# First cross attention: the output projection moves to the mix's PSUM bank, and a tile's order on three engines is changed

## The reference, cut to what matters

```python
x = x + tanh(g_xattn[1]) * _L1_xattn_ref(_layernorm(x), ctx, ctx, mask, wq, bq, wk, bk, wv, bv, wo, bo)

def _L1_xattn_ref(q, k, v, mask, wq, bq, wk, bk, wv, bv, wo, bo):   # 16 heads of 8
    qh, kh, vh = (split_heads(a @ w.T + b) for a, w, b in ((q, wq, bq), (k, wk, bk), (v, wv, bv)))
    corr = einsum('bhqd,bhkd->bhqk', qh, kh) / sqrt(8)
    corr = where(row_mask, corr, -1e9)          # a masked row gets even weights
    hidden = einsum('bhqk,bhkd->bhqd', softmax(corr), vh)
    return hidden.reshape(B, S, 128) @ wo.T + bo
```

## Time and profile before

| | us |
|---|---|
| median of 3 runs (3789.99 to 3798.97) | 3791.75 |
| the profiled execution's own time | 3789.1 |
| its span in the profile | 3787.0 |
| TensorE matmul busy | 3182.0 (84%) |
| VectorE busy | 2670.9 (71%) |
| ScalarE busy | 1691.3 (45%) |
| GpSimd busy | 1309.2 (35%) |

### The profile page before, as it was taken

One profiled execution on the slowest core, in us unless ns is written; L12 is line 12 of the kernel. 1 busy time (PEld: TensorE's weight loads), 2 busy tenths in 40 slices (PEclk: granted clock), 3 DMA queues, 4 the chain that ended last, 5 costly groups with the idle time before them and its releaser, 6 DMA issues. The chain is left out here.

```text
span 3787.0 us, 91181 instructions
## 1 busy us (share of the span) xinstructions
PE 3182.0 (84%) x31627; PEld 2212.8 (58%) x31627; DVE 2670.9 (71%) x5541; ACT 1691.3 (45%) x3176; POOL 1309.2 (35%) x1592
## 2 busy tenths in 40 slices
PE   3687999998888893699859997489999778999886
PEld 1465787886666441566646664256666445666644
DVE  7666555555788779788766666778887547888655
ACT  1232223222777355555512223256666225666521
POOL 1664100000233000144310003078887108898710
PEclk8776999999999996799959999799999899999998
DMA  4211000000000015011000002200000110000011
GB/s 134 65 43 52 0 0 0 0 0 5 14 14 14 1 58 208 16 46 45 28 17 1 0 0 66 62 13 10 9 10 4 36 30 12 10 9 9 9 33 55
DMA packets 164346, 107.86 MB, mean 28 GB/s; under 512 B 91486, under 2 KB 153100, under 8 KB 163212
## 3 DMA queue, kind: packets, MB, share of 16 engines
q1 hardware_dynamic: 162652, 104.02, 9.3%
q10 hardware_dynamic: 1584, 2.44, 0.2%
HBM read 68.52 MB, written 16.78 MB: 23 GB/s over the span
## 5 line engine op out<-in xcount | busy, mean ns | idle before, releaser
L2478 POOL TENSOR_TENSOR la_turned<-la_turned,la_sines 128x1024 f32<-128x1024 f32 x128 | 301.8, 2358 | 152.3 <-DVE la_sines L2406 149.4
L2398 DVE TENSOR_TENSOR la_turned<-A,la_cos 128x1024 f32<-128x1024 f32 x128 | 156.8, 1225 | 163.6 <-ACT la_sq L2377 146.9
L2472 POOL TENSOR_TENSOR la_scaled<-la_turned,la_rlen 128x1024 f32<-128x1024 f32 x128 | 243.6, 1903 | 16.9 <-POOL la_rlen L2465 13.4
L916 PE MATMUL B<-l0f_mixed,l0f_sums 128*128 128x256 f32 x768 | 176.2, 379 | 0.0
L1386 POOL COPY l1x_vd<-half 128x16 f32<-128x16 f32 x8 | 1.2, 212 | 490.9 <-POOLq L48 490.9
L2715 ACT ACTIVATE gg_gate<-B,gg_b 128x512 f32<-128x512 f32 (+1 forms) x96 | 65.9, 686 | 211.6 <-PE B L2741 211.6
L2509 PEld LDWEIGHTS A<-ident,la_scaled 128*128 128x128 f32 x1024 | 119.9, 141 | 66.0 <-issue 65.7
L916 PEld LDWEIGHTS B<-l0f_mixed,l0f_sums 128*128 128x128 f32 x768 | 145.9, 190 | 19.8
L2524 PE MATMUL A<-la_wq,la_hT 128*128 128x512 f32 x256 | 148.4, 662 | 10.9 <-DVE la_sines L2406 10.9
L1717 POOL TENSOR_SCALAR l3x_factor<-l3x_raw 128x256 f32<-128x256 int32 x16 | 13.8, 864 | 398.3 <-DMA l3x_raw<-in_l3x_mask 397.1
L2411 DVE TENSOR_REDUCE la_length<-la_sq 128x16 f32<-128x1024 f32 x128 | 151.0, 1180 | 0.0
(11 more groups left out here) (465 smaller groups left out, 9215.3 us busy)
## 6 DMA issues: line engine op xcount, KB each, us to landing
l1f_spill<-l1f_work SPq DMA_DIRECT2D x16, 768.0 KB, 3.3
l1f_xT<-l1f_spill SPq DMA_DIRECT2D x16, 768.0 KB, 6.0
l2x_ctx<-in_ctx SPq DMA_DIRECT2D x128, 64.0 KB, 2.2
memory_vd<-vd SPq DMA_DIRECT2D x64, 68.0 KB
X<-in_x SPq DMA_DIRECT2D x4, 1024.0 KB, 6.2
gates_rows<-in_ctx_rows SPq DMA_DIRECT2D x16, 256.0 KB, 2.9
memory_ctxT<-in_ctxT SPq DMA_DIRECT2D x64, 64.0 KB, 1.8
l1x_ctxT<-in_ctxT SPq DMA_DIRECT2D x64, 64.0 KB
```

What stands on the lines that cost most here:

```text
L916: last = pe.matmul(bank[:, o * H:o * H + H], weights[:, k, o * P:o * P + P], x[:, k], start=(k == 0), stop=(k == 1))
L2398: dve.tensor_tensor(heads(turned[j % 2][:]), made_heads, cos[:, :, None, :].broadcast_to([P, 2, HEADS3, W3]), ALU.mult)\
L2472: pool.tensor_tensor(by_head(scaled), by_head(turned), spread_heads(rlen[j % 2][:], W3), ALU.mult)\
L2478: pool.tensor_tensor(turned[j % 2][:], turned[j % 2][:], sines[j % 2][:], ALU.add)\
```

## The change

y_out moves from `inputs` to `mixes`, behind turned_o. The waits that kept project_o and update apart from x_in, k_out and v_out go (update on q_set, set_q on out_done, turn_x on added, project_o on values). In their place the mix of a tile waits until the update of the tile before it is done (`added`, `done(it, j, 1)`), as both are now at the bank `mixes`. The order of a step becomes:

- TensorE: scores t, turn_o t-3, turn_x t+2, make_kv t+2, project_o t-3, turn_p t-1, mix t-2, project_q t+2.
- VectorE: outputs t-3, shift t, update t-3, measure t-3, norm_x t+3.
- ScalarE: copy_o t-3, copy_x, set_k and keep_v t+2, copy_p t-1, set_q t+2, exps t.

```diff
--- before.py
+++ after.py
@@ -1353,7 +1353,7 @@
         turned_p, mixes, inputs = m.B[0], m.B[1][:, 0:CH], m.B[1][:, CH:2 * CH]
         out = mixes[:, 0:G * NW].rearrange("p (h w) -> p h w", h=H)
         if projected:
-            turned_o, y_out = mixes[:, G * NW:G * NW + P], inputs[:, P:2 * P]
+            turned_o, y_out = mixes[:, G * NW:G * NW + P], mixes[:, G * NW + P:G * NW + 2 * P]
         else:
             turned_o, y_out = inputs[:, P:2 * P], inputs[:, 2 * P:3 * P]
         x_in, k_out, v_out = inputs[:, 0:P], inputs[:, P:2 * P], inputs[:, 2 * P:3 * P]
@@ -1448,8 +1448,6 @@
                     t = it * 4 + j
                     dve.wait_ge(out_done, done(it, j))
                     dve.wait_ge(moved, done(it, j))
-                    if projected:
-                        dve.wait_ge(q_set, ahead(it, j, 5))
                     dve.scalar_tensor_tensor(m.X[:, t, :], y_out, m.tanh_g[:, gate_at:gate_at + 1], m.X[:, t, :],
                                              ALU.mult, ALU.add).then_inc(added, 1)
 
@@ -1480,12 +1478,12 @@
 
                 def step(it, j):
                     if projected:
-                        at4(it, j, -4, update)
+                        at4(it, j, -3, outputs)
                     at4(it, j, 0, shift)
+                    at4(it, j, -3, update)
                     if not projected:
-                        at4(it, j, -3, update)
-                    at4(it, j, -2, outputs)
-                    at4(it, j, -4 if projected else -3, measure)
+                        at4(it, j, -2, outputs)
+                    at4(it, j, -3, measure)
                     at4(it, j, 3, norm_x)
 
                 steps4(dve, step)
@@ -1530,7 +1528,6 @@
                     act.wait_ge(q_made if projected else turned, done(it, j))
                     act.wait_ge(scored, done(it, j, 2))
                     if projected:
-                        act.wait_ge(out_done, done(it, j, 5) if not isinstance(it, int) else max(done(it, j, 5), BEFORE))
                         act.activation(qT[j % 2][:], x_in, ACT.Identity, bias=bq[:]).then_inc(q_set, 1)
                     else:
                         act.copy(qT[j % 2][:], x_in).then_inc(q_set, 1)
@@ -1541,16 +1538,16 @@
 
                 def step(it, j):
                     at4(it, j, -3, copy_o)
-                    if not projected:
-                        at4(it, j, 2, set_q)
-                    at4(it, j, -1, copy_p)
                     if projected:
                         at4(it, j, 2, copy_x)
                         at4(it, j, 2, set_k)
                         at4(it, j, 2, keep_v)
+                        at4(it, j, -1, copy_p)
+                        at4(it, j, 2, set_q)
+                    else:
+                        at4(it, j, 2, set_q)
+                        at4(it, j, -1, copy_p)
                     at4(it, j, 0, exps)
-                    if projected:
-                        at4(it, j, 2, set_q)
 
                 steps4(act, step)
 
@@ -1589,7 +1586,8 @@
                 def turn_x(it, j):
                     pe.wait_ge(normed_x, done(it, j))
                     pe.wait_ge(q_set, done(it, j, 1))
-                    pe.wait_ge(added, done(it, j, 6) if not isinstance(it, int) else max(done(it, j, 6), BEFORE))
+                    if not projected:
+                        pe.wait_ge(added, done(it, j, 6) if not isinstance(it, int) else max(done(it, j, 6), BEFORE))
                     pe.transpose(x_in, xn[j % 2][:], m.ident[:]).then_inc(turned, 1)
 
                 def make_kv(it, j):
@@ -1610,6 +1608,8 @@
                 def mix(it, j):
                     pe.wait_ge(values, done(it, j))
                     pe.wait_ge(o_copied if projected else o_done, done(it, j, 1))
+                    if projected:
+                        pe.wait_ge(added, done(it, j, 1))
                     pe.wait_ge(p_copied, done(it, j))
                     for g in range(G):
                         for b in range(2):
@@ -1620,7 +1620,8 @@
 
                 def project_o(it, j):
                     pe.wait_ge(o_copied, done(it, j))
-                    pe.wait_ge(values if projected else q_set, ahead(it, j, 5))
+                    if not projected:
+                        pe.wait_ge(q_set, ahead(it, j, 5))
                     pe.wait_ge(added, done(it, j, 1))
                     pe.matmul(y_out, oT[j % 2][:], wo[:], start=True, stop=True).then_inc(out_done, 1)
 
@@ -1635,16 +1636,16 @@
                 def step(it, j):
                     at4(it, j, 0, scores)
                     at4(it, j, -3, turn_o)
-                    if not projected:
-                        at4(it, j, 2, turn_x)
+                    at4(it, j, 2, turn_x)
+                    if projected:
+                        at4(it, j, 2, make_kv)
+                        at4(it, j, -3, project_o)
                     at4(it, j, -1, turn_p)
-                    if projected:
-                        at4(it, j, 2, turn_x)
-                        at4(it, j, 2, make_kv)
                     at4(it, j, -2, mix)
                     if projected:
                         at4(it, j, 2, project_q)
-                    at4(it, j, -3, project_o)
+                    else:
+                        at4(it, j, -3, project_o)
 
                 steps4(pe, step)
```

## The result

The changed kernel takes 3889.47 us, the median of 4 runs (3886.32 to 3891.37), against 3791.32 before: a ratio of 1.0254, with a 95% interval of 1.0236 to 1.0272. The forecast was 3857 with a range of 3834 to 3880. So it is slower, as forecast, but by 98 us and not by 65, and 9 us outside the range.

A forecast was written before the change was run, and what follows sets the result against it. TensorE's queue plus its 0.76 us wait for keep_v set the 4.79 us step; the new closed chain adds 1.05 over 59 steps (62 us), the end about 3: +65, forecast 3857 us, range 3834 to 3880.

The forecast's parts named there:

- The chain: Scores, maximum, subtraction, update, mix, keep_v, project_q, scores: 5.84 us a tile against 4.79, 62 us over 59 steps.
- The handover to the mix: From VectorE's update to TensorE's mix: TensorE starts 0.05 us after VectorE's end, as turn_o did after L1444.
- The clock: Rival 2, TensorE's clock falls in the stage: 71 us more, 3928; chance 0.10 in whole or part.
- a clock lower for a fifth of the time: Partial case of rival 2 in the changed stage: total 3871 us; within rival 2's chance of 0.10.
- The end: Step 62 and last two passes, where mix through update no longer overlap: about 3 us more.
- about 1: In step 62 the scores of 63 wait for update and mix too: about 1 us.
- Rival 1: ScalarE's chain alone sets the step at 5.4 to 5.7 us: about 3840; chance 0.08.
- Rivals 3 and 4: 3: wait met early, VectorE's freed 0.75 counts, 3756, chance 0.03; 4: new waits fall into idle time, about 3792, 0.02.
- What was hidden: Outputs ahead of shift, measure, norm_x, turn_x, make_kv, project_o: covered by waiting; outputs would add 0.54 a tile if uncovered.
- VectorE's freed 0.75: Update no longer waits for set_q, freeing 0.75 us a step; alone worth nothing, VectorE then waits for scores.
- The rule on the bank: Mix and update may not be at one bank at once, so the wait stays and 5.84 stands.

The follow-up runs named there:

- The added instruction: Changed kernel with one more VectorE tensor_scalar (128x128, to an unread tile) between subtraction and update: 3909.51 us, ratio 1.0303.
- the wait order: Changed kernel with the mix's wait for the update put behind its wait for copy_p: 3876.83 us, ratio 1.0220.
- The second of the kernels with mix early: Kernel before, TensorE's mix moved ahead of turn_x, make_kv, turn_p, project_q; ScalarE copy_p, set_q, exps: 3838.96 us, ratio 1.0125.
- the fill: Changed kernel with the first four of turn_p's eight transposes done twice in each step: 3872.52 us, ratio 1.0207.
- a ScalarE circle shorter by 1 us: Changed kernel with ScalarE's copy_p ahead of keep_v again: 3897.19 us, ratio 1.0278.
- the version that won: Kernel before, TensorE turn_x, make_kv, mix, turn_p, project_q, project_o; ScalarE exps t-1 after copy_o, set_q ahead of copy_p: 3753.57 us, ratio 0.9909.

## Why the prediction was right and wrong

*The chain.* Right: the closed chain scores, maximum, subtraction, update, mix, keep_v, project_q is what sets the step at the full clock, and it was forecast at 5.84, measured 6.02 to 6.12. The added instruction lengthened it by the time from its start to the update's, and the update ahead of shift shortened it to 5.56. Not shown is what the bank and its wait cost apart from the new order of the engines' steps: no run has one without the other.

*The handover to the mix.* Mis-sized: "TensorE starts 0.05 after VectorE's end", taken from turn_o at the end of the stage. Inside the loop it measured 0.26, of which the wait order gave back 0.11. With mix to keep_v 1.15 for 1.11, the step grew by 1.27 in the mean instead of 1.05: 75 for 62 us.

*The clock.* This is the step of the prediction that failed: it added up a stage at the clock 1.00. The price of a clock lower for a fifth of the time was there (3871), with 0.10 for all such cases. The argument against it, TensorE 74% busy at 1.00 in another stage and no gap over 1 us, did not carry over: here it was about 80% busy by the profile (80.47 of 100 us, stretched by slow matmuls), the longest wait of TensorE in the loop was 0.77 us, and the clock was 0.88. Even at the full clock the profile has TensorE busy for 77% of a step (4.64 of 6.02), not the 69% that came of its 4.03. The clock cost 16 us in the loop, and about 5 of the 7 us by which the end was longer than forecast. The Trainium skill (TensorE: Matmul & The Clock Gate, section "A second HAM failure mode: psum-queue depth-cycling") tells of frequent short waits between groups of matmuls with the clock going back and forth, in a bf16 kernel that cycles through PSUM banks. The trace agrees: granted clock 0.88, scores of 0.69 and 1.16 us in turn. I had given it too small a chance.

Which trait of the step brings the clock down stays open. The second of the kernels with mix early has a step about as long (5.66), TensorE about as busy, and the clock at 0.99; here the whole stretch from 960 to 1250:

```profile
960.00:1250.00 290.00, 235.03 (x3662) 178.98 (x3661) 221.93 (x453) 174.76 (x408) 75.27 (x102) 0.99 0.04 12
```

TensorE waits there mostly once a step, 0.84 us at the mix, and 0.2 at project_q; in the changed kernel it waits 0.5 at the mix and 0.75 at project_q. No run varied that by itself.

*The end.* 3 us forecast, 10 measured. With the clock held by the fill, it is (4.83 - 3.74) + (16.9 - 12.7) = 5.3; the first term is the forecast "about 1".

*The sum.* The 32 us between forecast and result are 13 of the chain, 16 of the clock in the loop and 7 of the end, less some 4 in the rest. Without the 21 of the clock it would have come out near 3868, without the 13 of the chain near 3876, both inside the range: the miss took both.

*Rival 1*, ScalarE's chain: it lies beside, as held; a ScalarE circle shorter by 1 us changed no full-clock step. *Rivals 3 and 4*: no sign.

*What was hidden.* Outputs, measure, norm_x, turn_x, make_kv, project_o: no wait in the list names them with weight, except project_o for copy_o, 8.5 us over 36 tiles, inside the time in which TensorE would wait at the mix anyway. VectorE's freed 0.75 shows as part of its 1.4 of waiting at the row maximum; no run tested its worth by itself.

*The rule on the bank.* The Trainium skill (PSUM — Partial Sum Buffer, section "PSUM bank collisions raise a hardware error") was the reason to hold that the wait can't be had for less. No run tried it without the wait, so the trace neither shows nor refutes it.

## What to carry to other kernels

When a buffer moves to another bank, the wait that comes with it closes a loop through the queues: walk from the waiting instruction to everything behind it on its engine, and back to what it waits for, and add up from start to start before counting what the old waits gave free. Put long work that others need not wait for (here maximum and subtraction, or exps) behind the short handovers on the same engine; the version that won is such a change of order, with exps of the tile before and with turn_p between mix and project_q, and the bank as it was. And when a forecast step leaves TensorE waiting several times in each step, price the clock in: here a step longer by 26% brought 16 us of slower matmuls on top, and a rearrangement that saved 0.5 us a step at the full clock saved nothing in the total.

## What the runs showed of the hardware that I had not expected

- Needless TensorE work made the kernel faster: four more transposes a tile, 17 us less, clock 0.89 to 0.99.
- A wait that has long been met is not free when it stands behind the one that comes last: 0.11 us on TensorE inside the loop.
- VectorE's tensor_scalar from SBUF to SBUF had a median of 0.52 us, with 0.22 at the shortest and 1.10 at the longest. In the rows above it starts at 1186.73, while GpSimd's tensor_tensor runs from 1186.63 to 1187.67, and ends at 1187.75, after 1.02 us. The next one starts at 1193.79 and ends at 1194.18, GpSimd's at 1194.09. In both it ended 0.1 after GpSimd's instruction, as if held until then. It is so in all 59 of its 64 rows that overlap one of GpSimd, with 0.07 to 0.09 between the ends; the five without GpSimd last 0.22 each. The Trainium skill (SBUF — State Buffer, section "Who interferes with whom") says that VectorE in its faster two-port mode and GpSimd share a pair of ports, and that the one that comes second waits until the first is done. These rows agree, each time with GpSimd's instruction started first. That both meet at the ports is the page's reason; the rows show only the times.
